# The query's rotary sum kept in PSUM, a router of summing and one-input steps, and earlier roots on GpSimd

## The reference

```
x = x + 0.5 * ffn(layernorm(x))
x = x + attention(layernorm(x))
x = x + 0.5 * ffn(layernorm(x))
```

```
kv    = einsum('bhtd,bhtv->bhdv', k_feat, v)
denom = max(einsum('bhtd,bhd->bht', q_feat, k_feat.sum(t)), 1e-6)
out   = einsum('bhtd,bhdv->bhtv', q_feat, kv) / denom @ W_out
```

```
probs     = sigmoid(x @ router.T)
topw, sel = top_k(probs, 2)
topw      = topw / (topw.sum(-1) + 1e-20)
combine   = sum(topw * onehot(sel))          # tokens x 8
h         = square(relu(x @ W1e));  y = h @ W2e
out       = einsum('td,te->td', y, combine)
```

## Time and profile before

| what | value |
|---|---|
| median of 3 runs (lowest to highest) | 851.85 us (851.54 to 852.6) |
| the profiled execution | 851.46 us |
| its span, first to last instruction | 849.6 us |
| TensorE busy | 741.7 us, 87% |
| VectorE busy | 676.8 us, 80% |
| ScalarE busy | 586.8 us, 69% |
| GpSimd busy | 689.8 us, 81% |
| granted TensorE clock, mean | 0.98 |

### The profile page before, as it was taken

One profiled execution on the slowest core, in us unless ns is written; L12 is line 12 of the kernel. 1 busy time (PEld: TensorE's weight loads), 2 busy tenths in 40 slices (PEclk: granted clock), 3 DMA queues, 4 the chain that ended last, 5 costly groups with the idle time before them and its releaser, 6 DMA issues.

```text
span 849.6 us, 14271 instructions
## 1 busy us (share of the span) xinstructions
PE 741.7 (87%) x3648; PEld 593.1 (70%) x3648; DVE 676.8 (80%) x1882; ACT 586.8 (69%) x1187; POOL 689.8 (81%) x666
## 2 busy tenths in 40 slices
PE   1677887878999999989899998989999989889787
PEld 1456665757777777878687776878777877667555
DVE  3656888898989898898879897998989687786553
ACT  3457585767785877787587767787767857657655
POOL 3478777779989899999799897999989877667776
PEclk9899899999999999999999999999999999899999
DMA  5443132033323221232333221333323303213330
GB/s 167 153 147 99 52 101 100 1 101 101 101 100 113 78 78 61 99 112 100 115 100 113 100 73 41 101 111 100 112 101 113 101 13 101 63 50 113 113 113 25
DMA packets 31019, 79.34 MB, mean 93 GB/s; under 512 B 3296, under 2 KB 14304, under 8 KB 30944
## 3 DMA queue, kind: packets, MB, share of 16 engines
q1 hardware_dynamic: 28672, 76.03, 27.3%
q10 hardware_dynamic: 2272, 2.51, 0.9%
HBM read 73.81 MB, written 4.72 MB: 92 GB/s over the span
## 4 chain that ended last, share of the span: by engine, by line
PE 35%; DVE 22%; POOL 17%; issue 16%; DMA 5%; ACT 4%; DVEq 0%; POOLq 0%; ACTq 0%; SPq 0%
POOL h_lo L876 9%; PE bank L506 5%; PE bank L508 4%; PE bank L507 4%; PE bank L524 4%; PE bank L525 4%; PE bank L526 4%; DVE hid L1049 4%; DMA g_all_f<-rows_f 3%; POOL root_f L870 3%; PE bank L620 2%; DVE bn_f L945 2%; PE bank L487 2%; DVE qa L1078 1%; ACT h_hi L753 1%
## 5 line engine op out<-in xcount | busy, mean ns | idle before, releaser
L876 POOL TENSOR_TENSOR h_lo<-hid,h_hi 128x512 fp32r<-128x512 f32 x384 | 497.2, 1318 | 96.1 <-ACT h_hi L753 95.7
L1049 DVE SCALAR_TENSOR_TENSOR hid<-bank,g_all_f 128x512 f32<-128x512 f32 x384 | 261.7, 682 | 105.6 <-PE bank L508 68.1
L742 ACT ACTIVATE hid<-hid 128x512 f32<-128x512 f32 x384 | 229.7, 624 | 68.8 <-DVE hid L1049 66.8
L753 ACT ACTIVATE h_hi<-hid 128x512 fp32r<-128x512 f32 x384 | 225.9, 621 | 4.9 <-ACT hid L742 0.8
L506 PE MATMUL bank<-x_hi_f,w_hi 128*128 128x512 f32 x384 | 167.8, 437 | 35.6 <-DVE hid L1049 28.6
L524 PE MATMUL bank<-h_hi,w_hi 128*128 128x512 f32 x384 | 156.0, 406 | 9.6 <-ACT yT L764 7.8
L525 PE MATMUL bank<-h_lo,w_hi 128*128 128x512 f32 x384 | 154.0, 401 | 0.0
L526 PE MATMUL bank<-h_hi,w_lo 128*128 128x512 f32 x384 | 153.6, 400 | 0.0
L508 PE MATMUL bank<-x_hi_f,w_lo 128*128 128x512 f32 x384 | 153.6, 400 | 0.0
L507 PE MATMUL bank<-x_lo_f,w_hi 128*128 128x512 f32 x384 | 153.2, 399 | 0.0
L506 PEld LDWEIGHTS bank<-x_hi_f,w_hi 128*128 128x128 f32 x384 | 74.0, 193 | 70.7 <-DVE hid L1049 44.0
(11 more groups left out here) (103 smaller groups left out, 1120.1 us busy)
## 6 DMA issues: line engine op xcount, KB each, us to landing
g_all_f<-rows_f SPq DMA_DIRECT2D x128, 512.0 KB, 5.7
x_sb<-in_x SPq DMA_DIRECT2D x16, 256.0 KB, 3.8
out_x<-x_sb SPq DMA_DIRECT2D x16, 256.0 KB, 7.2
g_all_f<-in_w ACTq DMA_DIRECT2D x2, 768.0 KB, 7.6
con<-in_const ACTq DMA_DIRECT2D x1, 652.0 KB, 7.7
rows_f<-g_row_f SPq DMA_DIRECT2D x32, 16.0 KB, 1.4
g_all_f<-in_wqkv ACTq DMA_DIRECT2D x1, 192.0 KB, 9.6
wout_sb<-in_wout ACTq DMA_DIRECT2D x1, 64.0 KB, 6.8
```

The lines of the kernel that those rows point to most:

```text
L742: fn(h, h, ACT.Square).then_inc(s_sq[s], 1)
L753: fn(h_hi[:, c, :], hid[:, c % STAGE, :], ACT.Copy).then_inc(s_hhi[s], 1)
L876: gp.tensor_tensor(h_lo[:, c, :], hid[:, c % STAGE, :], h_hi[:, c, :].bitcast(F32), ALU.subtract).then_inc(s_hlo[s], 1)
L1049: v.scalar_tensor_tensor(hid[:, c % STAGE, :], hp[c % 2][:], 0.0, g_all[s][:, EXPERT[c], :], ALU.max, ALU.mult).then_inc(s_z[s], 1)
```

## The change

The query's sum stays in bank a1: the sine product is written back to it, the sum is made there, and `exp` and `qf` read it there (`q_sum`). So `state`, which writes a1, now waits for `qf`, and `q_features` moves up, directly behind `k_features`. `odds` is made by ScalarE behind `ex`. `best` gets a leading column that holds 1e-20; `tot` is one `tensor_reduce` over three columns; the factor 2 falls away and comes back as `scale=0.5` in the copy of `yT`. `cwt` is made by an instruction that also writes a sum (`accum_out`), which nothing reads. The mask `g_top` falls away: the row copy subtracts 2e-19 and takes the positive part (Relu), which turns the root of the floor `TINY` (1.2e-38) into zero. `g_tok` becomes a `tensor_reduce` over the two picks. The searches, `tot`, `rtot`, `cw` and `cwt` come some chunks sooner on VectorE, and `root_of_weights` two chunks sooner on GpSimd.

```diff
+        q_sum = a1[:].rearrange("p (b t) -> p b t", b=BG)
...
                 pe.wait_ge(A["kf"], value(n + 1))
+                pe.wait_ge(A["qf"], value(n + 1))
...
-                pe.wait_ge(A["qf"], value(n + 1))
                 pe.wait_ge(A["kvs"], value(n + 1))
...
                 fn(ex[s][:], l, ACT.Exp, scale=-1.0).then_inc(s_ex[s], 1)
+                if due(n):
+                    act.wait_ge(s_prob[s], value(n))
+                act.wait_ge(s_ex[s], value(n + 1))
+                fn(odds[s][:], ex[s][:], ACT.Identity, bias=c_one[:, 0:1]).then_inc(s_odds[s], 1)
...
-                fn(g_row[s][:], tp[0:EXP * TG, 0:P], ACT.Copy).then_inc(s_gr[s], 1)
+                fn(g_row[s][:], tp[0:EXP * TG, 0:P], ACT.Relu, bias=c_cut[0:EXP * TG, 0:1]).then_inc(s_gr[s], 1)
...
-                fn(yT[:], yp[s][:], ACT.Copy).then_inc(s_yT[s], 1)
+                fn(yT[:], yp[s][:], ACT.Copy, scale=0.5).then_inc(s_yT[s], 1)
...
-                    fn(eq[:], qa[:], ACT.Exp, bias=minus_one[:, 0:1]).then_inc(A["eq"], 1)
+                    fn(eq[:], q_sum, ACT.Exp, bias=minus_one[:, 0:1]).then_inc(A["eq"], 1)
...
-                remainders(t, 2, 3, 4, 5, 6, 7)
+                remainders(t, 2, 3, 4, 5, 6)
+                root_of_weights("f1", t + 2)
+                remainders(t, 7)
                 low_part("at", t - 1, 0)
-                remainders(t, 8)
-                root_of_weights("f1", t + 2)
-                remainders(t, 9, 10)
+                remainders(t, 8, 9, 10)
...
-                remainders(t, 16, 17, 18, 19)
+                remainders(t, 16, 17, 18)
+                root_of_weights("f2", t + 2 - SHIFT)
+                remainders(t, 19)
                 inv_std("f2", t + 3 - SHIFT)
                 remainders(t, 20)
-                root_of_weights("f2", t + 2 - SHIFT)
...
+            v.memset(best["f1"][:, :, 0:1], 1e-20)
+            v.memset(best["f2"][:, :, 0:1], 1e-20).then_inc(s_floor, 1)
...
-                    v.tensor_scalar(odds[s][:], ex[s][:], 1.0, None, ALU.add).then_inc(s_rt[s], 1)
...
-                    v.tensor_tensor(tot[s][:], best[s][:, :, 0], best[s][:, :, 1], ALU.add).then_inc(s_rt[s], 1)
-                    v.tensor_scalar(tot[s][:], tot[s][:], 1e-20, 2.0, ALU.add, ALU.mult).then_inc(s_rt[s], 1)
+                v.tensor_reduce(tot[s][:], best[s][:, :, 0:1 + TOPK], AX.X, ALU.add).then_inc(s_tot[s], 1)
...
-                    v.tensor_scalar(cwt[s][:], cw[s][:], TINY, None, ALU.max).then_inc(s_cw[s], 1)
+                    v.tensor_scalar(cwt[s][:], cw[s][:], TINY, 0.0, ALU.max, ALU.add, accum_out=cw_sum[s][:]) \
+                        .then_inc(s_cwt[s], 1)
...
-                    v.scalar_tensor_tensor(g_top[s][:], cw[s][:], 0.0, root[s][:], ALU.is_gt, ALU.mult) \
-                        .then_inc(s_gm[s], 1)
...
-                    v.tensor_tensor(g_tok[s][:].rearrange("p e k -> p k e"), pick[s][:, :, 0], pick[s][:, :, 1], ALU.add) \
-                        .then_inc(s_gt[s], 1)
+                    v.tensor_reduce(g_tok[s][:].rearrange("p e k -> p k e"), pick[s][:].rearrange("p k i e -> p k e i"),
+                                    AX.X, ALU.add).then_inc(s_gt[s], 1)
...
-                v.tensor_tensor(qb[:], a1[:].rearrange("p (b t) -> p b t", b=BG), sin_q, ALU.mult).then_inc(A["qb"], 1)
+                v.tensor_tensor(q_sum, q_sum, sin_q, ALU.mult).then_inc(A["qb"], 1)
...
-                v.scalar_tensor_tensor(qa[:], qa[:], 1.0, qb[:], ALU.add, ALU.add).then_inc(A["xq"], 1)
+                v.scalar_tensor_tensor(q_sum, q_sum, 1.0, qa[:], ALU.add, ALU.add).then_inc(A["xq"], 1)
...
-                    v.scalar_tensor_tensor(qf[:].rearrange("p (b t) -> p b t", b=BG), eq[:], 1.0, qa[:], ALU.min, ALU.max) \
+                    v.scalar_tensor_tensor(qf[:].rearrange("p (b t) -> p b t", b=BG), eq[:], 1.0, q_sum, ALU.min, ALU.max) \
```

More of the change, by code:

```diff
@@ L59 @@
 TINY = 1.2e-38
+ROOT_CUT = 2e-19
 KVW = D + HEADS
@@ L244, in build @@
         odds = {s: sb(f"odds_{s}", [P, TG, EXP]) for s in FFN}
-        best = {s: sb(f"best_{s}", [P, TG, EXP]) for s in FFN}
+        best = {s: sb(f"best_{s}", [P, TG, 1 + EXP]) for s in FFN}
         which = {s: sb(f"which_{s}", [P, TG, EXP], mybir.dt.uint32) for s in FFN}
@@ L317, in build @@
         s_ex = per("ex", FFN)
-        s_rt = per("rt", FFN)
+        s_odds = per("odds", FFN)
+        s_prob = per("prob", FFN)
+        s_best = per("best", FFN)
+        s_which = per("which", FFN)
+        s_tot = per("tot", FFN)
+        s_rtot = per("rtot", FFN)
+        s_cw = per("cw", FFN)
+        s_cwt = per("cwt", FFN)
         s_chosen = per("chosen", FFN)
-        s_cw = per("cw", FFN)
         s_root = per("root", FFN)
-        s_gm = per("gm", FFN)
+        s_pick = per("pick", FFN)
         s_gt = per("gt", FFN)
@@ L976, in pick_two, with where_two @@
[L976 removed]
+                dve.wait_ge(s_prob[s], value(n + 1))
+                dve.sem_inc(s_gate, 1)
+                for k in range(TG):
+                    i = v.max(best[s][:, k, 1:], prob[s][:, k, :])
+                i.then_inc(s_best[s], 1)
+            def where_two(s, n):
                 if not live(n):
                     return
[L980 to L989, removed]
[L990 to L999 removed]
@@ new lines, in where_two @@
+                dve.wait_ge(s_best[s], value(n + 1))
+                dve.sem_inc(s_gate, 1)
+                v.tensor_reduce(tot[s][:], best[s][:, :, 0:1 + TOPK], AX.X, ALU.add).then_inc(s_tot[s], 1)
+                for k in range(TG):
+                    i = v.max_index(which[s][:, k, :], best[s][:, k, 1:], prob[s][:, k, :])
+                i.then_inc(s_which[s], 1)
+                dve.wait_ge(s_tot[s], value(n + 1))
+                v.reciprocal(rtot[s][:], tot[s][:]).then_inc(s_rtot[s], 1)
@@ L1005, in weigh_two, with choose_two @@
                 if step == 0:
-                    dve.wait_ge(s_rt[s], value(n * RSTEPS + RSTEPS))
-                    v.reciprocal(rtot[s][:], tot[s][:]).then_inc(s_cw[s], 1)
+                    dve.wait_ge(s_rtot[s], value(n + 1))
+                    v.tensor_tensor(cw[s][:], best[s][:, :, 1:1 + TOPK], rtot[s][:].unsqueeze(2).to_broadcast([P, TG, TOPK]),
+                                    ALU.mult).then_inc(s_cw[s], 1)
                 elif step == 1:
-                    dve.wait_ge(s_cw[s], value(n * 3 + 1))
-                    v.tensor_tensor(cw[s][:], best[s][:, :, 0:TOPK], rtot[s][:].unsqueeze(2).to_broadcast([P, TG, TOPK]),
-                                    ALU.mult).then_inc(s_cw[s], 1)
-                elif step == 2:
-                    dve.wait_ge(s_cw[s], value(n * 3 + 2))
-                    v.tensor_scalar(cwt[s][:], cw[s][:], TINY, None, ALU.max).then_inc(s_cw[s], 1)
+                    dve.wait_ge(s_cw[s], value(n + 1))
+                    v.tensor_scalar(cwt[s][:], cw[s][:], TINY, 0.0, ALU.max, ALU.add, accum_out=cw_sum[s][:]) \
+                        .then_inc(s_cwt[s], 1)
+            def choose_two(s, n):
+                if not live(n):
+                    return
+                dve.wait_ge(s_which[s], value(n + 1))
+                v.tensor_tensor(chosen[s][:], which[s][:, :, 0:TOPK].unsqueeze(3).to_broadcast([P, TG, TOPK, EXP]),
+                                expert, ALU.is_equal).then_inc(s_chosen[s], 1)
             def spread_roots(s, n, step):
```

82 lines of the change are left out of this document (32 added, 50 removed).

## The result

The changed kernel takes 826.62 us in the median of four runs (823.68 to 828.62), against 851.69 (850.72 to 852.6) for the kernel before in four: a ratio of 0.9691, with an interval of 0.966 to 0.9722. That is a gain of 25 us. The time lies 13.6 us above the predicted 813.0: inside the range of 792 to 836, but outside the 803 to 823 that the forecast gave to its own mechanism.

What follows compares the result with a forecast made beforehand. TensorE was taken to hold the pace, with some 81 us of visible waiting, mostly on VectorE. Gains of 16 (full turns), 14 (first stretch), 6 (last) and 2.5 (start) sum to 38.5: 851.46 to 813.0 us, range 792 to 836.

Steps and rivals of the forecast that it cites:

- the lock: VectorE operations with two SBUF inputs, or in fast one-input mode, wait out the running GpSimd instruction; PSUM-operand or reciprocal-like ones don't.
- stay as slow as they are: On VectorE, `cw`, `chosen`, `pick`, the casts and the key's sum keep their durations while 117.5 us go elsewhere.
- The rival by which the forms still wait (829 us): One-input sums, accumulator form or PSUM sum still wait for GpSimd on VectorE: gain 22 us, 829; chance 0.08.
- VectorE writing PSUM, taken at nothing: The query's sine product, now written to PSUM, costs nothing extra; bound 0.68 x 16 = 11 us.
- The full stretch, 16 forecast: Turns with both routers: `kvm` waits of 5.8 us go, and half of 20.5 before up products: 16 us.
- The first stretch, 14 and 2.5 for the start forecast: Before 193 us: 0.6 of 26.7 us of VectorE waits, 16, less 2 for `x_lo_at`; start 2.5 from first `odds`.
- 0.65 of it: After 664 us: 11 of 16.9 us of VectorE waits go, less 1.8 for `qf` and 3 for `x_lo_at`: 6.
- taken as even in front of the first `hid`: A turn's first `hid` gets 0.6 us of `qf` in front and loses 0.5 of `rtot`, `cw`, `cwt`: even.
- a lost cover (0.6 x 16): If the three chunks ahead of `state` no longer cover its wait for `qf`, the cost is 10 us.
- no wait: Sign of the forecast: with `root` two chunks sooner on GpSimd, VectorE no longer waits for `root`.
- The slower rival (a root ahead of `x_lo_at`): At the query projection: late `x_lo_at` costs TensorE up to 26 us, 15 of gain left: 862; chance 0.04.
- GpSimd as the next bound (831 us): Full turns: GpSimd takes over and `hid` waits for `h_lo`; full stretch gives 5 instead of 16: 831; chance 0.25.

Runs made afterwards that it cites:

- x2: The kernel before with the query's rotary part alone (sum in PSUM, new place of `qf`): 846.79 us, 0.9934.
- x5: The changed kernel with `tot` and `g_tok` made again by two-input sums and `cwt` by the plain form: 846.96 us, 0.9911.
- x8: The changed kernel with every turn written out instead of looping: 816.50 us, 0.9561.
- x1: The changed kernel with the query's sum and `qf` as before, in SBUF and in the old place: 821.63 us, 0.9629.
- x3: The changed kernel with `q_features` put in front of `k_features`, PSUM sum kept: 816.42 us, 0.9558.
- x7: The changed kernel with the query's sum in SBUF again but the new order of `qf` kept: 836.28 us, 0.9786.
- x10: The changed kernel with `q_features` first, and f1's root put behind `x_lo_at`: 821.46 us, 0.9605.
- x9: The changed kernel with every turn written out instead of looping and `q_features` first: 806.56 us, 0.9456.

## Why the prediction was right, and where its sizes were off

The direction, the lock and the list of waits that go were right; the size was not. Of 38.5 us forecast 28.1 came in the profiled execution and 25 in the median: 15.8 of 16 in the full stretch, 10.8 of 16.5 before it, 1.5 of 6 behind it. The time fell nearer to two rivals, 829 and 831 us, whose mechanisms the runs refute (below), so the number alone would have misled. One figure of the working is a slip: 64 us are the waits for VectorE alone, and with the unnamed ones they are 70; the forecast's terms don't use it.

**VectorE's busy time, 117.5 us less forecast, 88.5 measured.** Every named term held or did better: `g_top` 27.8, `odds` 17.9 and the second `tot` 14.1 went; `tot` gave 15.9 for 15.6, `g_tok` 10.6 for 11.0, `cwt` 13.5 for 10.6 (6.7 us are left, its read-out of 78 ns included), the query's two lines 20.5 for 20.5; 120.3 in all. The step that failed was "stay as slow as they are", said of `cw`, `chosen`, `pick`, the casts and the key's sum: `cw`, `chosen`, `pick` and the cast of `x_hi_f` took back 25.8 us and `kf` 4.7, while the key's sum gave 3.9; 26.6 net of the 31.8 between 120.3 and 88.5. The rest is spread over small differences and overlaps of records. x2 shows it at its plainest, 20.5 us removed and 5 gained.

**The lock's reading** stands: both new forms have maxima of 167 and 227 ns, three operations with a PSUM operand never exceed 693, and x5 brings waits of up to 1493 back by changing only the form. The Trainium skill (SBUF — State Buffer, Who interferes with whom) says that `tensor_reduce` and the accumulator form of `tensor_scalar` don't contend with GpSimd; the runs agree, at 20 us (x5). The rival by which the forms still wait (829 us) was wrong. VectorE writing PSUM, taken at nothing, took 687 ns in the median against 681 at the fastest for SBUF.

**The full stretch, 16 forecast, 15.8 measured, by another split.** `kvm`'s 5.8 us went to 0.3, as said. `hid` and its unnamed partner went from 20.5 to 11.9, 8.6 instead of 10.2. All waits fell by 12.6; the rest goes with TensorE's own busy time, 445.5 to 441.5 us, which the working had not counted on and no run explains. So the match of 15.8 with 16 is in part luck. That the loop's edge stays was said; that it grows was not: 2.9 us at most before, 3.34 and 3.52 now, and of the 11.1 us for `hid` 7.3 are gone in x8 (3.8 left). The ten turns average 45.5 us as forecast, but as eight of 44.7 and two of 48.8.

**The first stretch, 14 and 2.5 for the start forecast, 10.8 measured.** The start held: the first `prob` starts at 17.60 instead of 21.04 us and the first `hid` at 30.24 instead of 32.39, 2.2 us sooner for the 2.5 forecast. Behind it 8.6 us were gained, not 14. TensorE's waits for VectorE fell from 26.7 to 12.9 us, 13.8, near the 16 of the working; `x_lo_at` in front of the query projection cost 0.2, not 2. What was missed is the row of the others: `yT` and `h_lo` went from 7.0 to 11.7 us, 11.9 with `x_lo_at`. Where VectorE comes sooner, TensorE next waits for ScalarE's and GpSimd's part of the same chunk, and a third of the freed time goes there. So the waits fell by 8.9 us net (13.8 - 4.9), which covers the 8.6.

**The last stretch, 6 forecast, 1.5 measured.** The step that failed is "0.65 of it", taken of all 16.9 us of VectorE's waits. Half of these, 8.5, are `state`'s for `kf`, and what stands in front of `kf` is a chain that the change doesn't shorten: the key's sum, its exponential on ScalarE, then `kf`. Around one `state` of the changed kernel, from the timelines of VectorE and of TensorE:

```profile
699.59 0.69 DVE L1116 SCALAR_TENSOR_TENSOR ka<-ka,kb 128x512 f32<-128x512 f32 x1
701.07 1.52 DVE L1121 SCALAR_TENSOR_TENSOR kf<-kb,ka 128x512 f32<-128x512 f32 x1 [0.19 <-ACT kb L784]
702.51 0.67 DVE L1096 SCALAR_TENSOR_TENSOR qf<-eq,bank 128x512 f32<-128x512 f32 x1
...
703.28 2.06 PE L614 MATMUL bank<-v_sb,kf 128*128 128x129 f32 x8 [3.37 <-DVE qf L1096]
```

In the same turn of the kernel before (`ka` at 725.26 us) the lock was met by `ka` (1.43 us) instead of `kf` (0.68): it moved within the chain, and `qf` comes on top. From the start of `ka` to `state` it is 3.69 us, 3.17 before; the 0.6 charged for it was right there, and low over the last three turns from one attention product to the next, which take 103.5 us against 99.95 in x1, where `qf` isn't ahead of `state` (101.9 in x3): 1.2 each. A part of that is the clock: two of the three `state` products of the changed kernel there run at about half speed (2.06 us), none of x1's does (1.16 us each). What was gained is `g_tok`'s 3.8 us; the waits for other engines rose from 4.0 to 6.2 in return.

**The query's order, taken as even in front of the first `hid`.** It is not: `qf` behind `kf` sits behind a hole of 0.79 us in which it could have run, and pushes `hid` into TensorE's path in the full turns (0.33 us in the one shown). x7 prices the new order at 14.7 us with the SBUF sum; with the PSUM sum, x3 gets 10 us by two lines exchanged. The working's other half held: the chunks ahead of `state` cover it in the full turns, and it waits for `qf` only three times, all behind 637.5 us. The working's 10 us for a lost cover (0.6 x 16) has the size of x3's gain by coincidence, since that cover was not lost.

**Roots and `x_lo_at`.** VectorE's wait for the root fell from 17.1 to 7.6 us; "no wait" was too much. The slower rival (a root ahead of `x_lo_at`) was wrong: TensorE waits 0.2 us for `x_lo_at`, ScalarE waits 8.5 us more for it, and x10, which undoes that and puts the root later, gains nothing. GpSimd as the next bound (831 us) was wrong too: x9 reaches 806.56 with the same 684 us of GpSimd work, and TensorE has no wait for `h_lo` in its full turns. In the thin stretches it is there in part: TensorE's waits for `h_lo` went from 0.3 to 3.2 and from 1.2 to 4.0 us.

**ScalarE's price, 0.3 us for each `odds`,** was 323 ns; `ex` of the same size took 199 beside it. The row copy, now Relu with a bias pointer, takes 343 ns instead of 251.

The Trainium skill (ScalarE: Activation LUTs, What ACT_TABLE_LOAD costs) gives about 93 ns for each pointer operand; the row copy's 92 agree, though no run changes the pointer alone. There is still one table load, of 1283 ns, with Relu in the kernel.

Open: what holds VectorE for 3 us and more at the loop's edge. The rows say only "issue", and x8 shows only that it goes with the loop. Open is why TensorE's own busy time fell. Open too is whether x10's 5 us over x3 are real, and whether `odds` on ScalarE is worth its 2.7.

## What to carry to other kernels

Price an operation that waits for a lock by the whole chain of operations that want that lock: of 120 us taken out of VectorE, 30 came back in five of its neighbours. Then ask what the next wait is for: three better forms were worth 20 us inside the whole change, where the root they lead to also came sooner, and nothing on their own (1.0023). And in an engine's list put work that is ready into a wait, not behind it; one exchange of two lines gave 10 us between medians (5 between the profiled executions), where the query's whole part had given the kernel before 6.

## What the runs showed of the hardware

The loop's edge is a stall on VectorE that the wait list calls "issue", in front of the first operation of a trip, whichever that is: `kf` in the changed kernel, `qf` in x3. It takes 3.3 and 3.5 us in the changed kernel, from 1.9 (x5) to 3.9 us (x3) over all runs with the loop. Written out without the loop, two kernels (x8, x9) have none of it, at 10 us of 827 and of 816. The two edge turns cost 8.1 us more than two ordinary ones in the changed kernel, 12.7 in x3 and 3.7 in the kernel before, with stalls of 2.9. The rows of x3:

```profile
DVE qf L1096 <- issue: 7.5, 2, 3.9
```

The accumulator form of `tensor_scalar` is two instructions in the trace, 140 and 78 ns; both together are a third of the 630 ns that the plain form took with its waits. And the product behind the wait of 3.37 us ran at half the clock, in two windows of the changed kernel around it (columns as in the stretches above):

```profile
698.00:703.00 5.00, 1.67 (x7) 0.70 (x5) 4.78 (x8) 3.34 (x8) 4.51 (x7) 0.99 0.00 0
703.00:705.50 2.50, 2.21 (x9) 2.22 (x10) 1.74 (x5) 2.15 (x6) 0.71 (x1) 0.50 0.00 0
```

0.50 is the lower level, 1.2 GHz. `state`'s eight products take 2.06 us there and 1.05 at clock 1.00 in the full turns, so this wait of 3.37 us cost about 1 us more than its own length; of the three such waits of the last stretch two were followed by products of 2.06 us, and one by products of 1.28.
